# A language-model layer on one core: the gating of four tiles cut in four pieces, and new orders of work on three engines

## The chip, the cores and the metric

The kernel runs on one NeuronCore of a Trainium2 chip. The metric is the device time of one execution in microseconds, as the median of several runs. The core has five engines that run side by side, each taking its own instructions in order: TensorE (PE in the profile; its weight loads are PEld), VectorE (DVE), ScalarE (ACT), GpSimd (POOL) and SyncE (SP, which here only issues DMAs). They wait for one another through semaphores.

## The reference

8192 tokens (64 tiles of 128) pass through three stages; what is computed is this:

```python
h = concat(token_table[ids], cat_table[ids])                      # 256 columns
# linear attention within each of the 64 sequences of 128 tokens, 16 heads of 16
x1 = layernorm(h);  q, k, v = x1 @ W_qkv + b_qkv
pq, pk = elu(q) + 1, elu(k) + 1
h = h + einsum(pq, pk^T v) / (pq . sum(pk) + 1e-6)                # per sequence of 128 tokens
# mixture of 16 experts: cosine logits, those above zero are kept, or the best two
x2 = layernorm(h);  rw = gating(x2, sim_matrix, gates)
q, k, v = sum_e rw_e * x2 @ {q,k,v}_proj[e]
out = h + sum_e rw_e * (softmax(causal(q k^T / sqrt(128))) v) @ o_proj[e]
```

A sequence has 128 tokens, so one tile of 128 rows is one sequence. All of it is in float32; the large products are made of three products of a high and a low half.

## The kernel before

The kernel has three stages. The attention stage gathers the rows of a tile, normalises them, makes q, k and v, the linear attention, the sum `h2`, its normalised form `x2`, and the gating logits; it finds the best two experts of each token, counts how many tokens went to each expert, and scatters each row of `x2` twice, sorted by expert. The second stage multiplies the sorted rows by the experts' weights, and the third does the softmax attention and the output product. Only the attention stage is touched here.

That stage is software-pipelined. `run1` calls `step1` of each engine with c = -7 up to `LAST_STEP`, with no loop left in the program. In step c an engine works on several tiles: `i.shift(n)` is tile c + n. So in one step VectorE makes `phi` of tile c+3, the attention result and `h2` of tile c+2, the low half of the turned `x1` of tile c+4, the statistics of tile c+5, and gating for tiles that have come out. Each engine's order within the step is the order of the code, written out by hand, and `after(eng, step, tile)` waits until another engine has finished that step of that tile.

The ring that goes through every step is this: VectorE writes `roots_in` (L1149, L1150), GpSimd raises it to the power -1/2 (`roots`, L712), VectorE makes `centers` from it (L1102), ScalarE normalises `x1` and `x2` with both (L851, L858), TensorE turns `x1` (L1426), ScalarE copies it as the high half `x1_T` (L864), VectorE makes the low half `x1_lo` (L1124). Then, by VectorE's order and not by need, come the attention result `attn` (L1128), `h2` (L1135), its statistics (L1138, L1140) and the next `roots_in`.

A second ring: from `x1_lo` TensorE makes `qk_product` (L1446 for the bias and six times L1450), ScalarE reads it twice (`qk_negative` L841, `qk_exp` L845), and VectorE makes `phi` (L1108). ScalarE's two come ahead of its `x1_normed` of the next tile. TensorE makes `kv_product` (L1512) from `phi` and from ScalarE's copy `v_copied` (L880), VectorE masks it (`kv_masked`, two instructions at L1160 and L1162), and TensorE makes `attn_sums` from that (L1471). VectorE and ScalarE also split a weight a step (`weight_lo` L511, `weight_hi` L506).

Gating works on groups of four tiles (of two at the end). When the last logits of a group are there, `experts_chosen` runs in that step, `rows_counted` in the next, `rows_placed` in the one after, and in the fourth there is none. They stand in VectorE's order between `roots_in` and `kv_masked`. After `rows_placed` GpSimd scatters one tile a step. Beside this it gathers the rows of tile c+7.

The buffers: `h` has eight, `x2` has nine (`N_X2`), `stats` has four.

## Time and profile before

| | |
|---|---|
| time before, median of 3 runs | 1168.15 us (1163.3 to 1169.42) |
| time of the profiled execution | 1171.71 us |
| its span, first to last instruction | 1170.0 us |
| TensorE busy | 993.7 us (85%) |
| VectorE busy | 861.6 us (74%) |
| GpSimd busy | 703.9 us (60%) |
| ScalarE busy | 603.1 us (52%) |
| attention stage | from the start to about 456 us |
| expert stage | about 456 to 690 us |
| last stage | about 690 us to the end |

The profile gives for each engine its busy time, for each line of the kernel its instructions and what the engine waited for ahead of them, and a timeline. In a timeline a row is: start, duration, engine, line, operation, output and inputs, and in brackets how long the engine had been idle before it and which instruction released it ("issue": nothing that the profile shows). An instruction can start a little ahead of the end of the one before it on its engine, so it is the distance from start to start that adds up. A buffer is sometimes named after another tile that shares its memory: `wo_hi` and `wo_lo` are the attention weights in this stage, `split_hi` and `split_lo` the turned `x1`, `row_y` and `x` are `x1` or `x2`, `h` can be `h2`.

### The profile page before, as it was taken

How to read it: one execution, taken by the hardware profiler on the slowest of the kernel's cores; microseconds unless marked ns; L12 is line 12 of the kernel's file. 1: busy time of each engine (PE TensorE's matmuls, PEld its weight loads, DVE VectorE, ACT ScalarE, POOL GpSimd, SP SyncE). 2: the span in 40 equal slices, each digit the busy share in tenths (PEclk: the TensorE clock that was granted, in tenths of full speed). 3: DMA queues.
4: the chain of work that ended last, by engine and by line, in shares of the span. 5: the costliest groups of instructions: out<-in, count | busy, mean ns of one | idle time of the engine just before them, and what ended most of it. 6: DMA issues, size and time to landing. Idle time of an engine off the chain costs nothing.

```text
span 1170.0 us, 27470 instructions
## 1 busy us (share of the span) xinstructions
PE 993.7 (85%) x6831; PEld 897.0 (77%) x6832; DVE 861.6 (74%) x2889; ACT 603.1 (52%) x1569; POOL 703.9 (60%) x924
## 2 busy tenths in 40 slices
PE   0887888888888871889999959999999999999998
PEld 0675777677776761779898849999999999999997
DVE  2576888888878874645445428888888888888988
ACT  1454666666666640444344425555555555555554
POOL 5666666666666658200000037888888888888885
PEclk9988999999999985899999979999999999999999
DMA  7464333443333323677777752333333333333331
GB/s 204 129 180 123 109 111 124 128 131 118 106 106 110 100 84 128 192 225 235 233 238 229 235 166 82 91 90 90 90 90 91 92 90 90 90 90 90 90 88 35
DMA packets 132265, 149.80 MB, mean 128 GB/s; under 512 B 14708, under 2 KB 119650, under 8 KB 132196
## 3 DMA queue, kind: packets, MB, share of 16 engines
q1 hardware_dynamic: 112964, 97.59, 26.9%
q0 software_dynamic: 18080, 50.36, 14.5%
q10 hardware_dynamic: 1152, 1.05, 0.3%
q8 instruction: 29, 0.48, 0.2%
q14 instruction: 40, 0.33, 0.1%
HBM read 83.79 MB, written 78.88 MB: 139 GB/s over the span
## 4 chain that ended last, share of the span: by engine, by line
PE 25%; POOL 25%; issue 19%; DVE 18%; DMA 5%; ACT 4%; SPq 2%; POOLq 2%; another core or an unknown queue 1%; DVEq 0%; ACTq 0%
POOL row_y L813 6%; PE bank L1419 5%; PE bank L1421 5%; PE bank L1420 5%; PE bank L1426 4%; POOL x2T L798 4%; POOL qk_neg L798 4%; PE bank L1450 3%; POOL x2T L800 2%; POOL qk_neg L800 2%; POOL x2T L794 2%; DVE split_lo L1124 2%; POOL qk_neg L794 2%; DMA h<-in_L_tok_special_table,ids 2%; DVE h L1135 1%
## 5 line engine op out<-in xcount | busy, mean ns | idle before, releaser
L1419 PE MATMUL bank<-wo_hi,split_lo 128*128 128x256 f32 x1024 | 304.4, 297 | 12.8 <-DVE x L1356 6.1
L1421 PE MATMUL bank<-wo_hi,split_hi 128*128 128x256 f32 x1024 | 288.6, 282 | 0.0
L1420 PE MATMUL bank<-wo_lo,split_hi 128*128 128x256 f32 x1024 | 288.2, 281 | 0.0
L1419 PEld LDWEIGHTS bank<-wo_hi,split_lo 128*128 128x128 f32 x1024 | 194.0, 189 | 25.3 <-DVE x L1356 12.2
L1420 PEld LDWEIGHTS bank<-wo_lo,split_hi 128*128 128x128 f32 x1024 | 194.1, 190 | 0.0
L1421 PEld LDWEIGHTS bank<-wo_hi,split_hi 128*128 128x128 f32 x1024 | 193.4, 189 | 0.0
L935 ACT ACTIVATE h<-bank,rwo 128x256 f32<-128x256 f32 x256 | 107.6, 471 | 119.3 <-PE bank L1421 112.6
L813 POOL DMA_INDIRECT row_y<-sorted_y,pair_now x128 | 126.3, 987 | 36.7 <-issue 30.1
L806 POOL COPY pair_now<-pair_at 128x2 uint32 (+1 forms) x64 | 11.9, 186 | 211.0 <-SPq L596 210.9
L1356 DVE SCALAR_TENSOR_TENSOR x<-bank,rwo,x 128x256 f32<-128x256 f32 x256 | 109.0, 475 | 19.7 <-PE bank L1421 19.6
L1257 DVE TENSOR_TENSOR split_lo<-bank,split_hi 128x256 fp32r<-128x256 f32 x144 | 60.9, 424 | 82.3 <-ACT split_hi L897 81.3
L1356 DVE SCALAR_TENSOR_TENSOR qk_e<-bank,rwo,qk_e 128x256 f32<-128x256 f32 x256 | 109.1, 475 | 15.4 <-PE bank L1421 15.1
L1419 PE MATMUL bank<-wq_hi,split_lo 128*128 x288 | 111.1, 386 | 0.0
L712 POOL TENSOR_TENSOR roots<-roots_in,minus_half 128x3 f32<-128x3 f32 x67 | 59.7, 891 | 84.7 <-DVE roots_in L1150 82.7
L740 POOL DMA_INDIRECT sorted_x<-row_y,position_u x86 | 85.5, 994 | 25.9 <-issue 25.9
L1420 PE MATMUL bank<-wq_lo,split_hi 128*128 x288 | 98.4, 342 | 0.0
L1421 PE MATMUL bank<-wq_hi,split_hi 128*128 x288 | 98.3, 341 | 0.0
L897 ACT CAST split_hi<-bank 128x256 fp32r<-128x256 f32 x144 | 54.0, 375 | 72.1 <-PE bank L1426 71.5
L1450 PE MATMUL bank<-wo_lo,split_hi 128*128 128x512 f32 (+1 forms) x256 | 89.9, 351 | 0.0
L1450 PE MATMUL bank<-wo_hi,split_lo 128*128 128x512 f32 (+1 forms) x256 | 89.6, 350 | 0.0
L1450 PE MATMUL bank<-wo_hi,split_hi 128*128 128x512 f32 (+1 forms) x256 | 88.8, 347 | 0.0
L841 ACT ACTIVATE qk_neg<-bank 128x512 f32<-128x512 f32 x64 | 38.3, 598 | 82.3 <-PE bank L1450 70.2
(229 smaller groups left out, 2669.4 us busy)
## 6 DMA issues: line engine op xcount, KB each, us to landing
sorted_y<-row_y SPq DMA_DIRECT2D x36, 384.0 KB, 3.2
sorted_y<-w_attn SPq DMA_DIRECT2D x36, 384.0 KB, 3.2
row_x<-sorted_x SPq DMA_DIRECT2D x72, 128.0 KB, 2.6
h_rows<-h SPq DMA_DIRECT2D x64, 128.0 KB
row_x<-h_rows SPq DMA_DIRECT2D x64, 128.0 KB, 2.1
out_h<-row_x SPq DMA_DIRECT2D x64, 128.0 KB, 1.7
embed_table<-in_L_tok_token_table SPq DMA_DIRECT2D x10, 625.0 KB
embed_table<-in_L_tok_special_table SPq DMA_DIRECT2D x10, 623.0 KB
```

The lines of the kernel that those rows point to most:

```text
L712: pool.tensor_tensor(roots[:, row, :], roots_in[:, row, :], minus_half[:, 0:3], ALU.pow).then_inc(done["roots"], 1)
L740: pool.indirect_dma_start(out=sorted_x, out_offset=offsets(position_u[:, t, n:n + 1]), in_=x2[t % N_X2], in_offset=None).then_inc(scattere ...
L798: pool.tensor_tensor(acc[:, :], part[:, 0, :], acc[:, :], ALU.add).then_inc(o_pooled, 1)
L813: pool.indirect_dma_start(out=row_y[:, 2 * tile.p + n, :], out_offset=None, in_=sorted_y, in_offset=offsets(pair_now[tile.q][:, n:n + 1])) ...
L897: act.copy(split[tile.q][0][:, :, :].rearrange("p c t -> p (c t)"), ps_turn[tile.p][:, 0:C]).then_inc(done["pair_hi"], 1)
L935: last = act.mul(part[:, j, :], ps[:, j * C:(j + 1) * C], rwo[tile.p][:, e:e + 1])
L1257: dve.tensor_tensor(lo, ps_turn[tile.p][:, 0:C], hi.bitcast(F32), ALU.subtract).then_inc(done["pair_lo"], 1)
L1356: ins = dve.scalar_tensor_tensor(acc[j][:, :], src, weight, base[:, :], ALU.mult, ALU.add)
L1419: pe.matmul(ps, left[1][c], right[0][c], start=(c == 0), stop=False)
L1420: pe.matmul(ps, left[0][c], right[1][c], start=False, stop=False)
L1421: last = pe.matmul(ps, left[0][c], right[0][c], start=False, stop=(c == n - 1))
L1450: last = pe.matmul(ps[:, 0:hi - lo], turned[x][c], w_attn_s[w][:, c, lo:hi], start=False, stop=end)
```

## The change

The gating of a group is cut into four functions instead of three, in four steps: `experts_chosen` ends with the best values, the new `experts_numbered` finds their indices and makes the two masks, `rows_counted` keeps the counting, `rows_placed` is as before. Everything behind them moves one step later: the rank product on TensorE, the scatters on GpSimd, and the last step of the stage (`LAST_STEP`), which is one more. `N_X2` is ten instead of nine; the room comes from small tiles that now share memory with others. VectorE's order is new: `weight_lo` goes behind `centers` (a step later than ScalarE's half), `attn` ahead of `x1_lo`, the aggregation of the first statistics ahead of `h2`, `kv_masked` right behind `h2` and so ahead of the statistics of `h2` and of `roots_in`, and the first statistics of a tile are taken at the end of the step before. ScalarE makes `v_copied` ahead of `x1_T`. TensorE makes the logits ahead of turning `x1`, and `kv_product` ahead of `qk_product`.

```diff
-    N_X2, N_RAW = 9, 4
-    LAST_STEP = B + 2
+    N_X2, N_RAW = 10, 4
+    LAST_STEP = B + 3
@@ scatters_at
-                at = first + n + 2
+                at = first + n + 3
@@ ScalarE, step1: behind x2_normed, ahead of x1_T; removed from behind x2_T
+                tile = i.shift(3)
+                if tile.inside(B):
+                    after(act, "v_product", tile)
+                    after(act, "kv_product", tile.shift(-1))
+                    act.copy(vx[:, :, 0:P], ps_v[:, 0:C].rearrange("p (g n) -> p g n", g=G)
+                             ).then_inc(done["v_copied"], 1)
@@ VectorE, gating
-                last.then_inc(gate_own, gate_count("top_values"))
-                gate_wait("top_values")
+                last.then_inc(gate_own, gate_count(f"top_values {g}"))
+
+            def experts_numbered(g):
+                first, n = GROUPS[g]
+                tiles = slice(first, first + n)
+                gate_wait(f"top_values {g}")
                 for t in range(first, first + n):
                     last = dve.max_index(top_at[:, t, :], top[:, t, :], routing[:, t, :])
                 last.then_inc(gate_own, gate_count("top_indices"))
                 gate_wait("top_indices")
-                quad_done(dve, "rank_product", g - 1)
+                quad_done(dve, "position_index", g - 1)
                 (is_one, is_two)
+            def rows_counted(g):
+                quad_done(dve, "rank_product", g - 1)
                 (before_rows, top_two, counts)
@@ VectorE, step1
+                for n in weights_at(i.c - 1):
+                    weight_lo(dve, n)
                 (phi, den)
-                if ln1_tile.inside(B):
-                    rows_landed(dve, ln1_tile.c)
-                    dve.bn_stats(stats[:, 2 * i.p, :], h[ln1_tile.c % 8]).then_inc(done["ln1_stats"], 1)
                 (reciprocal)
-                (x1_lo)
                 (attn)
+                (x1_lo)
+                (bn_aggr of ln1_tile)
                 (h2)
+                (kv_masked: two tensor_tensor, after kv_product of phi_tile)
                 (bn_stats and bn_aggr of h2)
-                (bn_aggr of ln1_tile)
                 (roots_in)
-                for back, piece in ((2, rows_placed), (1, rows_counted), (0, experts_chosen)):
+                for back, piece in ((3, rows_placed), (2, rows_counted), (1, experts_numbered), (0, experts_chosen)):
-                (kv_masked)
-                for n in weights_at(i.c):
-                    weight_lo(dve, n)
+                if stats_tile.inside(B):
+                    rows_landed(dve, stats_tile.c)
+                    dve.bn_stats(stats[:, 2 * (1 - i.p), :], h[stats_tile.c % 8]).then_inc(done["ln1_stats"], 1)
@@ TensorE, step1: the order within a step
-   rank product (i.c - 2), attn_sums, turn x1, logits, turn phi, turn x2, qk_product, kv_product, v_product
+   rank product (i.c - 3), attn_sums, logits, turn x1, turn phi, turn x2, kv_product, qk_product, v_product
```

Words in brackets stand for code that is the same on both sides. `stats_tile` is `i.shift(6)`.

## Rows read from the trace of the kernel before

**Rows 1.** Busy time of each engine in two stretches; columns: stretch, length, engines, clock, DMA.
```profile
121.50:410.20 288.70, 244.73 (x1528) 203.77 (x1528) 239.24 (x1106) 184.14 (x421) 186.38 (x189) 0.99 0.37 114
90.00:109.00 19.00, 12.50 (x65) 10.34 (x66) 9.80 (x47) 7.54 (x17) 11.96 (x13) 0.82 0.45 135
```

**Rows 2.** The same view for L1108 (`phi`, once a step) alone: VectorE busy, count.
```profile
121.50:410.20 288.70, 32.12 (x47) 0.99 0.37 114
```

**Rows 3.** Who waited for whom, 121 to 410 us: total, times, longest.
```profile
POOL roots L712 <- DVE roots_in L1150: 64.3, 47, 2.4
```

**Rows 4.** Timeline of VectorE, one step without gating, from `centers` to `centers`.
```profile
244.61 0.15 DVE L1102 SCALAR_TENSOR_TENSOR centers<-moments,roots 128x2 f32<-128x2 f32 x1
...
245.28 0.17 DVE L1113 TENSOR_SCALAR den<-bank 128x16 f32<-128x16 f32 x1
245.37 0.42 DVE L1118 BATCH_NORM_STATS2 stats<-h 128x6 f32<-128x256 f32 x1
245.70 0.23 DVE L1121 RECIPROCAL zden<-den 128x16 f32<-128x16 f32 x1
246.46 0.42 DVE L1124 TENSOR_TENSOR split_lo<-bank,split_hi 128x256 fp32r<-128x256 f32 x1 [0.53 <-ACT split_hi L864]
246.80 0.41 DVE L1128 TENSOR_TENSOR attn<-bank,zden 128x256 f32<-128x256 f32 x1
247.35 0.43 DVE L1135 TENSOR_TENSOR h<-h,attn 128x256 f32<-128x256 f32 x1
247.81 0.43 DVE L1138 BATCH_NORM_STATS2 stats<-h 128x6 f32<-128x256 f32 x1
...
248.56 0.17 DVE L1149 TENSOR_SCALAR roots_in<-moments 128x2 f32<-128x2 f32 x1
...
249.45 0.43 DVE L1160 TENSOR_TENSOR kvm<-bank,head_mask 128x256 f32<-128x256 f32 x1 [0.67 <-PE bank L1512]
...
250.21 0.15 DVE L1102 SCALAR_TENSOR_TENSOR centers<-moments,roots 128x2 f32<-128x2 f32 x1
```

**Rows 5.** Timeline of VectorE: where the three gating functions begin and end.
```profile
229.84 0.15 DVE L1021 TENSOR_TENSOR energy<-roots 128x4 f32<-128x4 f32 x1
...
231.20 0.09 DVE L1038 MATCH_VALUE_LOAD top_at<-top,routing 128x8 f32 x1
...
231.80 0.40 DVE L1160 TENSOR_TENSOR kvm<-bank,head_mask 128x256 f32<-128x256 f32 x1
...
236.62 0.22 DVE L1048 TENSOR_TENSOR is_one<-expert_no,top_at 128x64 f32<-128x64 f32 x1
...
236.90 0.17 DVE L1055 CAST before_rows<-before_rows 128x16 fp32r<-128x16 f32 x1
...
238.05 0.41 DVE L1160 TENSOR_TENSOR kvm<-bank,head_mask 128x256 f32<-128x256 f32 x1
...
242.88 0.21 DVE L1072 TENSOR_TENSOR ranks<-bank,region_start 128x64 f32<-128x64 f32 x1
...
243.86 0.42 DVE L1160 TENSOR_TENSOR kvm<-bank,head_mask 128x256 f32<-128x256 f32 x1
```

**Rows 6.** Timeline of ScalarE in the step of rows 4.
```profile
244.86 0.60 ACT L851 ACTIVATE x<-h,centers,roots 128x256 f32<-128x256 f32 x1 [0.51 <-DVE centers L1102]
...
246.05 0.37 ACT L864 CAST split_hi<-bank 128x256 fp32r<-128x256 f32 x1
...
248.94 0.60 ACT L841 ACTIVATE qk_neg<-bank 128x512 f32<-128x512 f32 x1 [1.04 <-PE bank L1450]
249.56 0.63 ACT L845 ACTIVATE qk_e<-qk_neg 128x512 f32<-128x512 f32 x1
```

**Rows 7.** Timeline of TensorE and GpSimd in the same step.
```profile
247.03 0.47 PE L1446 MATMUL bank<-bias,ones_r 128*128 128x512 f32 x1 [0.18 <-DVE split_lo L1124]
...
248.87 0.88 POOL L712 TENSOR_TENSOR roots<-roots_in,minus_half 128x3 f32<-128x3 f32 x1 [1.14 <-DVE roots_in L1150]
```

**Rows 8.** Who waited for whom in the starting steps, 33 to 100 us.
```profile
POOL row_x L717 <- DMA row_x<-in_L_tok_special_table,ids: 4.9, 2, 2.6
```

More of the change, by code:

```diff
@@ L269, in build @@
         gates_shifted = wide[0]
+        top_two_f = moments[:, :, :, :].rearrange("p r n m -> p (r n m)")[:, 0:2 * B].rearrange("p (b n) -> p b n", n=2)
+        gap, gates_open = [centers[:, :, :].rearrange("p r n -> p (r n)")[:, n * B:(n + 1) * B] for n in range(2)]
         ids_rows_f, ids_low = qk_e[0:B, 0:T], x2T[:, 0:B]
@@ L875, in step1 @@
                     act.copy(x2T[:, :], ps_x2[:, 0:C]).then_inc(done["x2_T"], 1)
-                tile = i.shift(3)
-                if tile.inside(B):
-                    after(act, "v_product", tile)
-                    after(act, "kv_product", tile.shift(-1))
-                    act.copy(vx[:, :, 0:P], ps_v[:, 0:C].rearrange("p (g n) -> p g n", g=G)
-                             ).then_inc(done["v_copied"], 1)
                 for n in weights_at(i.c):
@@ L1039, in experts_chosen @@
                 last.then_inc(gate_own, gate_count("top_indices"))
-            def rows_counted(g):
-                first, n = GROUPS[g]
-                tiles = slice(first, first + n)
                 gate_wait("top_indices")
-                quad_done(dve, "rank_product", g - 1)
+                quad_done(dve, "position_index", g - 1)
                 numbers = over_quad(expert_no, n)
@@ L1121, in step1 @@
                     dve.reciprocal(zden[:, :, :], den[:, :, :]).then_inc(done["attn_z"], 1)
-                if x1_tile.inside(B):
-                    after(dve, "x1_T", x1_tile)
-                    dve.tensor_tensor(x1T_s[1], ps_x1[:, 0:C], x1T_s[0].bitcast(F32), ALU.subtract
-                                      ).then_inc(done["x1_lo"], 1)
                 if attn_tile.inside(B):
@@ L1131, in step1 @@
                                       ).then_inc(done["attn"], 1)
+                if x1_tile.inside(B):
+                    after(dve, "x1_T", x1_tile)
+                    dve.tensor_tensor(x1T_s[1], ps_x1[:, 0:C], x1T_s[0].bitcast(F32), ALU.subtract
+                                      ).then_inc(done["x1_lo"], 1)
+                if ln1_tile.inside(B):
+                    after(dve, "ln1_stats", ln1_tile)
+                    dve.bn_aggr(moments[:, ln1_tile.c, 0, :], stats[:, 2 * i.p, :]).then_inc(done["ln1_moments"], 1)
+                if attn_tile.inside(B):
                     landed_half(dve, h2_stored, attn_tile.shift(-2))
@@ L1472, in step1 @@
                     last.then_inc(done["attn_sums"], 1)
-                tile = i.shift(4)
-                if tile.inside(B):
-                    after(pe, "x1_lo", tile.shift(-1))
-                    after(pe, "x1_normed", tile)
-                    turn(ps_x1, *halves(x1)).then_inc(done["x1_turned"], 1)
                 if i.inside(B):
@@ L1489, in step1 @@
                     last.then_inc(done["logits_product"], 1)
+                tile = i.shift(4)
+                if tile.inside(B):
+                    after(pe, "x1_lo", tile.shift(-1))
+                    after(pe, "x1_normed", tile)
+                    turn(ps_x1, *halves(x1)).then_inc(done["x1_turned"], 1)
                 tile = i.shift(3)
@@ L1499, in step1 @@
                     turn(ps_x2, *halves(x2[tile.c % N_X2])).then_inc(done["x2_turned"], 1)
-                tile = i.shift(4)
-                if tile.inside(B):
-                    after(pe, "phi", tile.shift(-1))
-                    after(pe, "x1_lo", tile)
-                    if tile.c == 0:
-                        pe.wait_ge(setup_v, 6)
-                    attn_product(tile, ps_qk, 0, 2 * C, "qk_product")
                 tile = i.shift(3)
@@ L1514, in step1 @@
                     last.then_inc(done["kv_product"], 1)
+                tile = i.shift(4)
+                if tile.inside(B):
+                    after(pe, "phi", tile.shift(-1))
+                    after(pe, "x1_lo", tile)
+                    if tile.c == 0:
+                        pe.wait_ge(setup_v, 6)
+                    attn_product(tile, ps_qk, 0, 2 * C, "qk_product")
                 tile = i.shift(4)
```

48 lines of the change are left out of this document (22 added, 26 removed).

## The prediction

> **What bounds the kernel now.** I read the busy time by stretch first, then the waits, then the timeline of single steps. The change touches the attention stage alone; the stages from 456 us on are taken as they are. In the even part of the stage, 121.5 to 410.2 us, 47 steps pass in 288.7 us [rows 1, 2], so a step takes 6.14 us. No engine is full: TensorE is busy 244.7 us of it (85%), VectorE 239.2 (83%), ScalarE and GpSimd 184 to 186 (64%) [rows 1]. So a ring of waits sets the step. GpSimd waited for `roots_in` in every one of the 47 steps [rows 3]: the ring runs over VectorE's `roots_in`.
>
> In a step without gating VectorE needs 5.60 us from `centers` to `centers` (244.61 to 250.21) and stands still twice: 0.53 us ahead of `x1_lo`, which waits for ScalarE's copy of the turned `x1`, and 0.67 us ahead of `kv_masked`, which waits for TensorE [rows 4]. The first of these stands ahead of `attn`, `h2`, its statistics and `roots_in`, none of which need `x1_lo`. And the work is uneven: `experts_chosen` takes 231.80 - 229.84 = 1.96 us, `rows_counted` 238.05 - 236.62 = 1.43, `rows_placed` 243.86 - 242.88 = 0.98, and the fourth step has none [rows 5]. In the long steps VectorE has no second wait to hide the work in; in the fourth it stands idle.
>
> **VectorE's step after the change, from start to start.** I take the step of rows 4 and edit it.
> - It is 5.60 us to begin with.
> - `den` to `reciprocal` was 0.42 with the first statistics between them. Without them the reciprocal waits only for `den` (0.17 long, and a hop of about 0.04): 0.21. The statistics, now at the step's end, take 0.33 (245.37 to 245.70). Together +0.12.
> - `reciprocal` to the next was 0.76, with the wait. `attn` needs the reciprocal's end, 0.23 and a hop: 0.29. That is -0.47.
> - `x1_lo`, `attn`, `h2` took 0.34 + 0.55 = 0.89, where 0.55 is `h2` waiting for `attn`. In the new order `attn`, `x1_lo`, the small aggregation, `h2` take 0.34 + 0.34 + 0.10 = 0.78, for the other two cover the end of `attn`. That is -0.11.
> - `h2` to its statistics was 0.46 by dependence; `kv_masked` between them lets it be 0.34, and its own two instructions and the weight only change place: -0.12.
> - From the second `roots_in` (0.08 behind the first at 248.56) to `kv_masked` was 0.81, mostly the idle 0.67. Now the next instruction follows in about 0.07: -0.74.
> - `x1_lo` could start 1.85 us after `centers` by VectorE's own order (phi, weight, `den`, reciprocal, `attn` ahead of it). ScalarE's `x1_T` started 246.05 - 244.61 = 1.44 after `centers`, and `x1_lo` 0.41 behind it [rows 4, 6]. With `v_copied` put ahead, a copy of the size of L864 (0.37 long), `x1_T` goes to about 1.54 and `x1_lo` to 1.95. So +0.10 of waiting stays.
>
> The sum is 5.60 + 0.12 - 0.47 - 0.11 - 0.12 - 0.74 + 0.10 = 4.38 us and the gating piece of the step. The pieces: choosing to the best values 231.20 - 229.84 = 1.36; numbering 231.80 - 231.20 = 0.60 and the two comparisons 236.90 - 236.62 = 0.28, with two hops 1.0; counting 238.05 - 236.90 = 1.15; placing 0.98 [rows 5]. They are less equal than the words of the change say, but their sum over four steps is 4.49 and the mean 1.12. Nothing of VectorE's time hides them any more. So the mean step by VectorE is 4.38 + 1.12 = **5.50 us** (5.36 at the least, 5.74 at the most).
>
> **Who else could be last.** GpSimd: `roots` started 0.31 after `roots_in` and takes 0.88 [rows 4, 7]; `centers` may start some 1.25 us after `roots_in`. VectorE reaches it after 0.15, a piece of 0.98 or more and statistics of 0.33, thus 1.46. VectorE is later by 0.2 or more in every step, so the power is covered; in the old fourth step nothing but the wait for TensorE covered it.
>
> TensorE, `kv_product`: it needs `v_copied`, which ends some 1.7 us after `centers`, follows the turn of `x2`, and ends at about 2.5; `kv_masked` wants it at 2.76. It is covered by 0.3 us. This is the closest of the moved waits: behind it on VectorE stand the statistics of `h2` and `roots_in`, for which GpSimd waits.
>
> TensorE and ScalarE, the second ring: `x1_lo` to the start of `qk_product` 247.03 - 246.46 = 0.57, to `qk_negative` 248.94 - 247.03 = 1.91, to `qk_exp` 0.62, to `x1_normed` 0.54 (its 0.63 less the usual overlap), from there to `x1_T` 246.05 - 244.86 = 1.19 and 0.10 for `v_copied`, and 0.41 to `x1_lo` [rows 4, 6, 7]. That makes 5.34 us a step, 0.16 less than VectorE. `kv_product` ahead of `qk_product` costs this ring nothing, since it runs while TensorE waits for `x1_lo`. The logits ahead of the turn of `x1` run while it waits for `x1_normed`. TensorE's own work is 244.7 / 47 = 5.2 us a step as busy time, with overlapping matmuls in it, so it is no bound by itself but leaves little room.
>
> GpSimd's work is 186.4 / 47 = 3.97 us a step and some 0.8 us between its indirect DMAs [rows 1]: 4.8, covered. The scatters go one step later and the tenth `x2` buffer gives that step back, so ScalarE's wait for a free buffer has the same number of steps as before. SyncE's DMAs keep their places; the store of `h2` follows `h2`.
>
> **The sum.** In the even part 47 x (6.14 - 5.50) = 30.1 us are saved. The start: rows of the first tiles come in parts, and GpSimd waits up to 2.6 us for a DMA there [rows 8], so these steps gain nothing; the first statistics, now one step nearer to the DMA that they need, may wait in some of them. Between -1 and +5 us, I take +1. The steps between start and even part ran in part at the low clock, two of them in 19.0 us at a mean granted clock of 0.82 [rows 1]; I take a gain of 1 us there. The end: one more step, which holds almost no work, but the last groups are placed one step later while GpSimd has scatters queued: between 0 and 5.6 us (a whole step), I take 1. Together 30.1 - 1 + 1 - 1 = 29 us. The profiled execution took 1171.71 us, hence 1142.6; it lies 3.6 us above the median of the runs shown, hence **1139 us**.
>
> **A rule weighed.** While GpSimd raises the roots, VectorE runs gating instructions with two inputs in SBUF; in the new order it does so in four steps of four instead of three. In the trace the counting step shows no stretching: 1.43 us for `rows_counted` is the sum of its short instructions, beside a `roots` of the usual length [rows 5, 7]. The Trainium skill says (SBUF — State Buffer, SBUF: two separate sides) that VectorE with two SBUF inputs and a GpSimd instruction that reads SBUF exclude each other for a whole instruction. By that rule the fourth step would pay a `roots` too, and it is the third rival below; the trace speaks against it.
>
> **Rivals.**
> 1. The second ring or `kv_masked` is last (25%). Its margins are 0.16 and 0.3 us, and the hops in it were read from an order in which they were not tight. If each of its six hops is 0.07 us longer, the step is 5.75: 47 x 0.39 = 18 us, and the time is 1150.
> 2. VectorE's step is shorter than the sum, because satisfied waits cost it less than in the old order, and low-clock spells vanish with TensorE's pauses (15%). With 5.36 a step and 3 us for the spells the time is 1129.
> 3. VectorE and GpSimd exclude each other (3%): 0.88 us more in one step of four, 47 x 0.22 = 10 us back: 1149.
> 4. The early steps are held by the DMA of the small table (3%): each of about 14 steps loses the 2.6 us of rows 8, 36 us, which takes all the gain: 1175, slower. Its place is the first statistics at the step's end, its point is a landing more than a step after the issue. Against it: the statistics have one step more than the landing needs once VectorE and GpSimd run over two steps.
> 5. TensorE's clock falls more often (5%). Two steps in 19.0 us [rows 1] make 9.5 a step at the low clock, 4 us more than 5.5. From 8 such steps on, the gain is gone; with 12 the time is 1139 + 48 = 1187, slower. Against it: the granted clock is 0.99 over the even part [rows 1], and the change shortens TensorE's pauses.
> 6. The stage gets faster but the end takes it back, the scatters being late anyway (5%): within 0.5%.
>
> **Chances.** The forecast as it stands 44%, the rivals as given. The measurement of this kernel can tell about 0.5% (5.8 us) from no change. Faster by more: 0.87; within: 0.05; slower: 0.08. The range takes in rivals 1 to 3 and VectorE's own bounds: 1127 to 1156.
>
> **What would show it.** In the trace after, starts of `phi` 5.3 to 5.7 us apart in all four steps of a group, 22.0 us for the four. The idle time ahead of `x1_lo` at 0.1 us instead of 0.53, the one ahead of `kv_masked` gone, and VectorE busy for over 90% of the even part. GpSimd still waits for `roots_in`, but `centers` does not wait for GpSimd. If `kv_masked` or `phi` shows idle time with TensorE or ScalarE as its releaser, rival 1 holds; if the first statistics wait for a DMA in many steps, rival 4; if the clock row shows more low slices, rival 5. The prediction is wrong if the step stays above 5.9 us, that is, if one of the moved waits is as late as the one it replaces.

## The result and the profile after

The changed kernel took **1125.18 us** (median of 4 runs, 1122.11 to 1129.77), the kernel before 1167.62 us (4 runs, 1163.3 to 1169.42): ratio 0.9637, 95% interval 0.9597 to 0.9677. The forecast was 1139 us with 1127 to 1156 as its range, so the gain was larger than forecast and the time lies below the range. That number needs a caution: of the four later sessions in which the changed kernel ran, it took 1149 and 1157 us in two, every run of it, beside an unchanged kernel before. The experiments find out what it is exposed to there.

The page of the profiled execution of the changed kernel (1126.18 us, span 1124.4): first line of the page, then VectorE's and the clock's row in 40 slices.

```profile
span 1124.4 us, 27485 instructions
...
DVE  2578999999999746454544279999999999988798
...
PEclk9999999999999859999999789999999999999899
```

From its fifth slice to the end of the even part VectorE is busy for nine tenths and more of the time, where it was at eight before. The same stretch as [rows 1], from step 10's `phi` to step 57's: columns stretch, length, PE, PEld, DVE, ACT, POOL, clock, DMA. The second line is `phi` alone (the stretch's end catches one more than 47), the third the 19 us in which [rows 1] had a clock of 0.82.

```profile
109.64:361.60 251.96, 233.33 (x1533) 202.44 (x1532) 236.63 (x1106) 170.68 (x422) 184.51 (x189) 1.00 0.42 131
...
109.64:361.60 251.96, 32.35 (x48) 1.00 0.42 131
...
90.00:109.00 19.00, 15.40 (x90) 12.95 (x89) 15.03 (x72) 10.46 (x27) 12.92 (x13) 0.91 0.38 118
```

47 steps in 251.96 us are **5.36 us** a step instead of 6.14. VectorE is busy for 236.63 / 251.96 = 94% of it and TensorE for 93%. Who waited for whom in that stretch:

```profile
ACT qk_neg L840 <- PE bank L1456: 77.4, 47, 2.0
POOL roots L711 <- DVE roots_in L1163: 28.9, 46, 1.1
...
ACT x L850 <- DVE centers L1106: 0.7, 2, 0.4
```

VectorE, which stood 0.53 us ahead of `x1_lo` in the steps before, is all but gone from this list (0.3 us ahead of `phi`, in one step). GpSimd's wait for `roots_in` fell from 64.3 us [rows 3] to 28.9. One step of VectorE, to be read beside [rows 4]:

```profile
221.58 0.14 DVE L1106 SCALAR_TENSOR_TENSOR centers<-moments,roots 128x2 f32<-128x2 f32 x1
...
222.65 0.17 DVE L1119 TENSOR_SCALAR den<-bank 128x16 f32<-128x16 f32 x1
222.85 0.26 DVE L1123 RECIPROCAL zden<-den 128x16 f32<-128x16 f32 x1
223.14 0.42 DVE L1126 TENSOR_TENSOR attn<-bank,zden 128x256 f32<-128x256 f32 x1
223.49 0.42 DVE L1132 TENSOR_TENSOR split_lo<-bank,split_hi 128x256 fp32r<-128x256 f32 x1
223.82 0.17 DVE L1136 BATCH_NORM_AGGREGATE moments<-stats 128x2 f32<-128x6 f32 x1
223.91 0.39 DVE L1141 TENSOR_TENSOR h<-h,attn 128x256 f32<-128x256 f32 x1
224.22 0.42 DVE L1147 TENSOR_TENSOR kvm<-bank,head_mask 128x256 f32<-128x256 f32 x1
224.56 0.17 DVE L1149 TENSOR_TENSOR kvm<-bank,head_of_row 128x16 f32<-128x16 f32 x1
224.64 0.42 DVE L1154 BATCH_NORM_STATS2 stats<-h 128x6 f32<-128x256 f32 x1
...
225.45 0.15 DVE L1163 TENSOR_SCALAR roots_in<-moments 128x1 f32<-128x1 f32 x1
225.52 0.15 DVE L1020 TENSOR_TENSOR energy<-roots 128x4 f32<-128x4 f32 x1
...
226.77 0.41 DVE L1172 BATCH_NORM_STATS2 stats<-row_x 128x6 f32<-128x256 f32 x1
227.09 0.14 DVE L1106 SCALAR_TENSOR_TENSOR centers<-moments,roots 128x2 f32<-128x2 f32 x1
```

No instruction carries an idle time in brackets. From `centers` to `centers` it is 5.51 us, of which the choosing piece has 226.77 - 225.52 = 1.25.

That doesn't mean that VectorE never waits. An instruction of 256 columns is 0.42 us long here and the next one starts 0.34 after its start, so a wait of up to 0.08 us hides in the overlap. It is seen by the distance from the releasing instruction. ScalarE's copy and `x1_lo`, in the step above and in the next one:

```profile
223.09 0.37 ACT L869 CAST split_hi<-bank 128x256 fp32r<-128x256 f32 x1
...
228.58 0.37 ACT L869 CAST split_hi<-bank 128x256 fp32r<-128x256 f32 x1
...
228.57 0.42 DVE L1126 TENSOR_TENSOR attn<-bank,zden 128x256 f32<-128x256 f32 x1
228.98 0.42 DVE L1132 TENSOR_TENSOR split_lo<-bank,split_hi 128x256 fp32r<-128x256 f32 x1
```

`x1_lo` starts 0.40 us behind the start of the copy and 0.03 behind its end, in both steps and in each of the 47; it is the same 0.03 in the kernel before, where VectorE stood idle for it. So the copy still releases it. In the second step `attn` to `x1_lo` is 0.41 us instead of 0.34: 0.07 us of waiting. On the average of the even steps this hidden wait is 0.04 us. `phi` has one too. In the choosing step it starts 0.10 us behind the end of ScalarE's `qk_exp`, the least that any step of any of these kernels has, and about 0.08 later than VectorE could start it; that is 0.03 us on the average of all steps.

The two profiled executions, 1171.71 and 1126.18 us, differ by 45.5 us: 11.9 up to step 10 (`phi` at 121.55 and 109.64), 36.7 in the 47 even steps, 3.8 from there to the start of the last stage (687.12 and 634.69), and 6.8 lost in the last stage. Part of that is chance: three profiles of the kernel before have step 10 at 121.55, 113.00 and 115.18 and a last stage of 482.9, 488.3 and 481.3 us; three of the changed kernel have 109.64, 109.94 and 109.48, and 489.7, 488.2 and 489.1. The even part is the same in all: 6.142, 6.141 and 6.142 against 5.361, 5.360 and 5.362 us a step.

### The profile page after: what moved, and what is told of

Same layout as the page of the kernel before. It is cut to its first block, busy times and chain, and to the rows that moved or that the text cites. A ratio compares the mean times of both kernels' runs of the same rounds, so it can differ in the third digit from the quotient of the medians.

```text
span 1124.4 us, 27485 instructions
## 1 busy us (share of the span) xinstructions
PE 981.4 (87%) x6831; PEld 895.2 (80%) x6832; DVE 878.1 (78%) x2889; ACT 585.5 (52%) x1569; POOL 709.3 (63%) x924
## 4 chain that ended last, share of the span: by engine, by line
POOL 27%; DVE 23%; PE 22%; issue 18%; DMA 5%; SPq 2%; POOLq 2%; ACT 1%; DVEq 0%; ACTq 0%
POOL row_y L812 6%; PE bank L1425 6%; PE bank L1427 5%; PE bank L1426 5%; POOL x2T L797 4%; PE bank L1432 3%; POOL qk_neg L797 3%; DVE phi L1114 3%; DMA h<-in_L_tok_special_table,ids 2%; POOL x2T L799 2%; POOL qk_neg L799 2%; POOL x2T L793 2%; POOL qk_neg L793 2%; DVE kvm L1147 2%; DVE attn L1126 2%
## 5 line engine op out<-in xcount | busy, mean ns | idle before, releaser
L812 POOL DMA_INDIRECT row_y<-sorted_y,pair_now x128 | 128.8, 1006 | 36.7 <-issue 29.3
L739 POOL DMA_INDIRECT sorted_x<-row_y,position_u x80 | 79.8, 997 | 24.1 <-issue 23.8
```

Source lines behind the costliest of these rows:

```text
L739: pool.indirect_dma_start(out=sorted_x, out_offset=offsets(position_u[:, t, n:n + 1]), in_=x2[t % N_X2], in_offset=None).then_inc(scattere ...
L812: pool.indirect_dma_start(out=row_y[:, 2 * tile.p + n, :], out_offset=None, in_=sorted_y, in_offset=offsets(pair_now[tile.q][:, n:n + 1])) ...
```

## The experiments

Five sessions after that of the result, each on one chip; the second, third and fourth on the same one by its number. The kernel before took 1168.06, 1170.34, 1168.85, 1165.6 and 1168.11 us in them.

**The two halves of the change.** `orders_only` is the changed kernel with the old cut of the gating:

```diff
-                for back, piece in ((3, rows_placed), (2, rows_counted), (1, experts_numbered), (0, experts_chosen)):
+                for back, piece in ((2, rows_placed), (1, rows_counted), (0, experts_chosen)):
```

What hangs on the cut goes back with it (`LAST_STEP`, the scatters, the rank product); `N_X2` stays ten.

> The changed kernel with the gating back in three pieces (1.96, 1.43, 0.98 us and none). Theory, VectorE's own order sets each step and rings only fill up the short one: steps of about 6.2, 5.7, 5.3 and 5.3 us, 5.6 on average instead of 5.34, so 47 x 0.27 = 13 us more than the changed kernel: 1138 us. Rival, the rings through TensorE and ScalarE set the mean and the pieces only move work: the mean step stays at 5.3 to 5.4 and the time at 1125 us.

`pieces_only` is the kernel before with the new cut:

```diff
-                for back, piece in ((2, rows_placed), (1, rows_counted), (0, experts_chosen)):
+                for back, piece in ((3, rows_placed), (2, rows_counted), (1, experts_numbered), (0, experts_chosen)):
```

Here `N_X2` is ten too, and the rest moves a step later as in the change.

> The kernel before with the gating in four pieces and everything that moves with them, in the old orders. Theory: a piece of about 1.1 us in each step costs what it exceeds the 0.7 us of waiting for kv_product by, so the steps are about 6.1, 6.0, 5.9, 5.8, 5.96 on average instead of 6.14, 7 to 8 us less than before: 1160 us. Rival, the pieces were most of the gain: under 1145 us. Second rival, they gain nothing without the orders: 1167 us.

Measured: 1140.77 us (ratio 0.9767, 0.9748 to 0.9786; mean step 5.638) and 1151.08 us (0.987, 0.9841 to 0.9899; mean step 5.901). The orders alone bring 27.3 us, the pieces alone 17.0, and the whole change 42.1 in that session (one run, `after_again`, 1125.95; `before_again`, one run for its trace, took 1163.78): nearly the sum. For `pieces_only` the expectation was 9 us too high; it had put the steps at 6.1, 6.0, 5.9 and 5.8 us, and they were 6.07, 5.81, 5.89 and 5.82.

> The kernel before once more, for its trace. If the spells of low TensorE clock in the first 111 us (five in the first trace) belong to the kernel, there are three or more again, and the first 13 steps take about 88 us again (from phi at 33.75 to phi at 121.55). If they are chance, their number differs and the time to that point moves by 5 us or more.

> The changed kernel once more, for its trace. If the 12 us gained by step 10 belong to the change, phi of that step starts at about 110 us again; if they were chance of the clock, it moves by 5 us or more. The even steps take 5.34 us again. The last stage, 6.8 us longer than before in the first trace, comes back to within 2 us of the 482.9 us of before if its extra low-clock spell was chance.

In `orders_only` the four kinds of step take 6.15, 5.69, 5.32 and 5.26 us from `phi` to `phi`. VectorE's order without a piece is 4.26 us, the short wait for `x1_T` in it, so with 1.96, 1.43 and 0.98 it would be 6.22, 5.69, 5.24 and 4.26. The last two are longer than that: something else ends them. Two starts of `phi` in `orders_only` show it:

```profile
222.19 0.69 DVE L1109 SCALAR_TENSOR_TENSOR phi<-bank,qk_e 128x512 f32<-128x512 f32 x1
227.44 0.69 DVE L1109 SCALAR_TENSOR_TENSOR phi<-bank,qk_e 128x512 f32<-128x512 f32 x1 [0.21 <-ACT qk_e L844]
```

`phi` waits for ScalarE's `qk_exp`: that is the second ring of the prediction, measured at 5.25 us where it was put at 5.34. A long step can't be made up by a short one below it, and this is what the equal pieces are worth once the orders are new.

**VectorE or the second ring.** `dve_plus` adds one instruction of 0.42 us to VectorE's step, `stats_mid` puts the first statistics back where they stood:

```diff
+                    dve.bn_stats(extra[:, i.p, :], h[stats_tile.c % 8])
```

> The changed kernel with one more bn_stats of 256 columns on VectorE at the end of each step, into a tile that nobody reads. Theory, VectorE's own work is the step: the even steps grow by the 0.33 us that such an instruction takes from start to start, from 5.36 to 5.69 on average, and the time by 16 us. Rival, the ring through TensorE and ScalarE (5.27 us by the trace) sets it: under 0.15 us a step more.

```diff
@@ VectorE, step1
                 (phi, den)
+                if ln1_tile.inside(B):
+                    rows_landed(dve, ln1_tile.c)
+                    dve.bn_stats(stats[:, 2 * i.p, :], h[ln1_tile.c % 8]).then_inc(done["ln1_stats"], 1)
                 (reciprocal ... gating)
-                if stats_tile.inside(B):
-                    (the same for stats_tile)
```

> The changed kernel with the first statistics back between den and the reciprocal. It fills a gap of 0.12 us of VectorE, so by VectorE's work alone a step falls to 5.24 us. By the second ring (phi to x1_lo 1.45 us by VectorE's order, then 0.56, 1.91, 0.63 and 0.69 us through TensorE and ScalarE back to phi: 5.24) it makes phi to x1_lo 0.21 longer, and no step can be under 5.45. If both rules hold the average is 5.5, slower than the 5.36 of the changed kernel; if the first alone, 5.24.

`dve_plus` took 1140.44 us with a mean step of 5.664, 0.30 more for an instruction that takes 0.33 from start to start. The missing 0.03 is the wait ahead of `phi`, which is gone there; `x1_lo` still starts 0.03 us behind the end of ScalarE's copy in every step. So what closes the mean step is a mixed ring: `centers`, by ScalarE and TensorE to `x1_T` and `x1_lo` (1.89 us), then VectorE's own order to the next `centers`. VectorE's own way to `x1_lo` is only 0.06 us shorter there. `stats_mid` took 1132.27 us, and nearly all its steps are 5.44 to 5.47 us from `phi` to `phi`, whatever piece they hold (the longest has 5.57); its `phi` waits:

```profile
223.19 0.69 DVE L1114 SCALAR_TENSOR_TENSOR phi<-bank,qk_e 128x512 f32<-128x512 f32 x1 [0.20 <-ACT qk_e L844]
```

With 0.22 us more between `phi` and `x1_lo` (`den` to `reciprocal` is 0.42 instead of 0.20) the second ring is last in every step. Without them it is about 5.22 to 5.25 us, 0.1 below the changed kernel's mean. The margin isn't there in each step: in the changed kernel `phi` starts 0.10 us behind the end of `qk_exp` in the choosing, counting and placing steps (medians 0.10, 0.10 and 0.11), which is the least there is, and only behind a choosing step has it 0.28. `act_idle` and `act_ring` add a copy to ScalarE's step, at its end and between `v_copied` and `x1_T`:

```diff
@@ ScalarE, step1, in one at the end, in the other ahead of x1_T
+                if 0 <= i.c < B - 4:
+                    act.copy(x1T[:, :], zeros[:, :])
```

> The changed kernel with one more copy of 256 columns on ScalarE (0.27 to 0.4 us) at the end of its step, where it stands idle for 1.6 us waiting for qk_product. Both theories: no change, 5.36 us a step, 1125 us. If ScalarE's work were a bound, 0.3 us a step more.

> The changed kernel with the same copy between v_copied and x1_T. VectorE reaches x1_lo when x1_T is just ready, so the 0.27 us (start to start) come back as standing still ahead of x1_lo, in VectorE's row and in both rings: 5.6 to 5.65 us a step, 12 us more, 1137 us. If x1_T had slack (the prediction had x1_lo wait 0.10 us, so it had none either), no change.

They took 1156.96 and 1161.05 us in the third session, where late signals (below) disturb about half of the steps. The undisturbed ones are 5.50 and 5.32 us in `act_idle`, 5.82 and 5.64 in `act_ring`: 0.3 us for the same copy, only because of its place, and `x1_lo` stands idle for 0.29 us in `act_ring`. So `x1_T` has no slack, while the end of ScalarE's step has. The times of the whole runs say nothing here.

**The moved instructions of VectorE.** `attn_late` puts `x1_lo` ahead of `attn` again, `kvm_late` puts `kv_masked` behind the gating:

```diff
+                (x1_lo)
                 (attn)
-                (x1_lo)
```

> The changed kernel with x1_lo ahead of attn again. x1_T is ready 0.35 us after VectorE gets there, so it stands still, and h2 then waits for the end of attn (0.2): the even steps grow by 0.4 to 0.55 us, to 5.8 to 5.9, and the time by 19 to 26 us. If ScalarE's wait is hidden anyway, 0.1 us or less.

```diff
                 (h2)
-                (kv_masked)
                 (bn_stats and bn_aggr of h2, roots_in, gating)
+                (kv_masked)
```

> The changed kernel with kv_masked back behind the gating piece. VectorE's work is the same and kv_product is ready in both places, and attn_sums still has 0.3 us before den wants it: the same time within 0.1 us a step, 1121 to 1130 us. If the move of kv_masked was what took away the waits, 0.3 us a step or more slower.

`attn_late` took 1149.5 us, mean step 5.848. This is the wait of [rows 4], back again:

```profile
224.87 0.42 DVE L1126 TENSOR_TENSOR split_lo<-bank,split_hi 128x256 fp32r<-128x256 f32 x1 [0.44 <-ACT split_hi L869]
```

So `attn` ahead of `x1_lo` is worth 5.848 - 5.360 = 0.49 us a step, 23 us in all; the forecast had -0.47 for this wait. `kvm_late` took 1132.93 us, mean step 5.470, 0.11 more: `h2` to its statistics is 0.43 us there (222.34 to 222.77) where with one instruction between it could be 0.31. `kv_masked` ahead of `roots_in` is worth that little, if TensorE is on time.

**The same kernel, 30 us slower.** `filled_gaps` moves `bn_aggr` and half of `kv_masked` into short dependence waits; `after_timed` is the changed kernel beside it.

```diff
-                (bn_aggr of ln1_tile)
                 (h2, kv_masked's first instruction)
+                (bn_stats of h2)
                 (kv_masked's second instruction)
-                (bn_stats of h2)
                 (bn_aggr of h2)
+                (bn_aggr of ln1_tile)
```

> The changed kernel with two short instructions of VectorE moved into gaps of dependence: the second of kv_masked (0.08 us) between the statistics of h2 and their aggregation, the aggregation of the first statistics (0.09 us) between that and roots_in. VectorE's work falls from 5.36 to 5.19 us a step, the rings stay at 5.24 to 5.27. Theory with both bounds: 5.27 to 5.29 us a step, 3 to 4 us less than the changed kernel: 1121 us. By VectorE alone: 5.19, 8 us less. If the gaps were not free: no change.

> The changed kernel as it is, on the same chip as filled_gaps: 1125 us, and even steps of 5.36 us.

`filled_gaps` took 1150.91 us (0.9855, 0.9832 to 0.9878) and the changed kernel 1157.36 (0.9907, 0.9887 to 0.9928; 6 runs, 1154.79 to 1159.6). Both expectations fell. `filled_gaps` was 6.4 us below the changed kernel beside it (mean step 5.783 against 5.915), but in a session with late signals that can't be put down to the filled waits. The undisturbed steps of `after_timed` are the known 5.3 and 5.5 us, but others take 5.9 and 6.9; in them VectorE waits ahead of `kv_masked`, which it never did in the even part of the profile after. The fourth session was to tell whether `kv_masked`'s place is what pays. `kvm_late_timed` is `kvm_late` again, `vcopy_late` is this:

```diff
@@ ScalarE, step1
-                (v_copied)
                 (x1_T, phi_q_T, x2_T)
+                (v_copied)
```

> The changed kernel itself once more. Theory A (what made it 1157 us in the third job belongs to that job): 1125 us, steps of 5.3 and 5.4 us, and no wait of kv_masked for kv_product beyond 0.1 us. Theory B (the kernel has two levels, met by chance of the job): 1157 us, with steps of 5.9 to 6.9 us among steps of 5.3, each with kv_product's signal 2 us and more behind the start of its matmuls.

> The changed kernel with kv_masked moved from ahead of the second statistics to the end of VectorE's step. If TensorE's signals are on time in this job: 1133 us, as in the second job (mean step 5.47). If they are late in some steps, theory A says that a late kv_product signal of 1 to 1.5 us no longer stops roots_in and the gating, so this kernel is faster than the changed kernel in the same job: 1135 to 1142. Theory B (late signals cost whatever the order, since x1 turned and phi turned are late as well): as slow as the changed kernel, 1155 to 1165.

> The changed kernel with ScalarE's v_copied (0.39 to 0.42 us) put back behind the copies of x2, where it stood before. Nothing on VectorE's ring or the second ring waits for it unless kv_product becomes late: kv_product follows it on TensorE, and kv_masked follows kv_product on VectorE. Theory: kv_product is done about 1.2 us later in the step, and kv_masked waits up to 0.5 us for it: mean step 5.36 to 5.9, 1125 to 1150 us. Rival: the copy fits into ScalarE's idle time and nothing moves: 1125 us.

> The kernel before, for its trace on this chip: 1163 to 1170 us, mean step 6.14. Where TensorE's signals are late in this job, they are late here too, and cost little, since kv_masked stands last in VectorE's step.

Measured in that session: the changed kernel 1149.01 us (ratio 0.9852, 0.9825 to 0.9878), `kvm_late_timed` **1130.46** (0.9692, 0.9668 to 0.9716), `vcopy_late` 1185.57 (1.0184, 1.0143 to 1.0225), the kernel before 1168.15 with a mean step of 6.142. The changed kernel's step of 5.888 and VectorE in one of the bad ones:

```profile
230.77 0.43 DVE L1126 TENSOR_TENSOR attn<-bank,zden 128x256 f32<-128x256 f32 x1
231.53 0.42 DVE L1132 TENSOR_TENSOR split_lo<-bank,split_hi 128x256 fp32r<-128x256 f32 x1 [0.34 <-ACT split_hi L869]
231.87 0.17 DVE L1136 BATCH_NORM_AGGREGATE moments<-stats 128x2 f32<-128x6 f32 x1
231.96 0.39 DVE L1141 TENSOR_TENSOR h<-h,attn 128x256 f32<-128x256 f32 x1
233.45 0.42 DVE L1147 TENSOR_TENSOR kvm<-bank,head_mask 128x256 f32<-128x256 f32 x1 [1.09 <-remote]
```

and TensorE's matmuls for it ("remote": the profile has no record of the releasing signal; it is `kv_product`, L1511):

```profile
230.51 0.41 PE L1432 MATMUL bank<-ident,phi 128*128 128x128 f32 x2
...
231.01 0.64 PE L1511 MATMUL bank<-vx,phi 128*128 128x130 f32 x4
```

The matmuls end at 231.65 by their row, and `kv_masked` starts 1.80 us later. The cleanest view is one kernel in two sessions, `kvm_late` and `kvm_late_timed`, a step of each. TensorE's turn of `phi` and ScalarE's work around the copy `pqT` that reads it, first in the second session:

```profile
221.25 0.41 PE L1432 MATMUL bank<-ident,phi 128*128 128x128 f32 x2
...
221.51 0.37 ACT L869 CAST split_hi<-bank 128x256 fp32r<-128x256 f32 x1
221.78 0.38 ACT L874 COPY pqT<-bank 128x256 f32<-128x256 f32 x1
...
224.38 0.60 ACT L840 ACTIVATE qk_neg<-bank 128x512 f32<-128x512 f32 x1 [1.65 <-PE bank L1456]
```

then in the fourth:

```profile
221.86 0.40 PE L1432 MATMUL bank<-ident,phi 128*128 128x128 f32 x2
...
222.14 0.37 ACT L869 CAST split_hi<-bank 128x256 fp32r<-128x256 f32 x1
223.56 0.38 ACT L874 COPY pqT<-bank 128x256 f32<-128x256 f32 x1 [1.04 <-PE bank L1432]
...
225.02 0.60 ACT L840 ACTIVATE qk_neg<-bank 128x512 f32<-128x512 f32 x1 [0.51 <-PE bank L1456]
```

From the start of the turn to `pqT` it is 0.53 us in the one and 1.70 in the other; to `qk_neg` 3.13 and 3.16. TensorE started its work at the same times, and only the signals in the middle of the step came late. I worked out the same from the trace's records of the signals: how long after the last matmul's recorded end its signal came, over 121 to 361 us. "Seen" is how many of the signals have a record; some are missing, most of them in the traces with late ones, so "none late" holds for those seen. The last row is the trace that the prediction was worked from.

```
kernel (session)   turn of phi                kv_product                 mean step
                   seen   median  90%   most  seen   median  90%   most
changed (1)        45/45  0.01   0.01   0.01  45/45  0.01   0.01   0.01  5.360
kvm_late (2)       44/44  0.01   0.01   0.01  44/44  0.01   0.01   0.01  5.470
changed (3)        28/40  0.01   0.96   1.37  38/40  0.82   1.78   1.80  5.915
changed (4)        28/41  0.01   0.62   0.97  35/41  0.76   1.68   1.73  5.888
kvm_late (4)       34/44  0.13   0.58   1.27  44/44  1.35   1.42   1.52  5.484
vcopy_late (4)     27/38  0.01   0.01   0.01  28/37  0.01   0.01   0.04  6.393
before (4)         27/39  0.01   0.01   0.49  39/39  0.01   0.01   0.01  6.142
changed (5)        45/45  0.01   0.01   0.01  45/45  0.01   0.01   0.01  5.362
before (first)     31/39  0.01   0.01   0.56  39/39  0.01   0.01   0.01  6.142
```

In the fourth session `kv_product` is late by 1.35 us in the median with `kv_masked` last in the step, and that costs 5.484 - 5.470 = 0.01 us a step; it is late by 0.76 with `kv_masked` ahead of `roots_in`, and that costs 5.888 - 5.360 = 0.53. So it is by `kv_masked`'s place that the changed kernel pays for late signals, as theory A had it for `kvm_late_timed` (it was even less, 1130 for 1135 to 1142). Its other half, that only the third session has this level, was wrong: the changed kernel met its higher level again, as theory B had it for `after_fourth`. What makes the signals late is open: the kernel before has two late turns of `phi` and no late `kv_product` in the same session, the mean granted clock is 0.96 to 0.97 with and without them, and `kvm_late` has none in the second session on the same chip. The changed kernel itself ran on that chip in the two sessions with late signals only; that it is the session and not the chip is known from `kvm_late` alone.

`vcopy_late` failed in the other direction, by more than the 0.5 us of its expectation, with TensorE's signals on time. One step of it, ScalarE, TensorE, VectorE:

```profile
227.71 0.41 ACT L879 COPY vx<-bank 128x256 f32<-128x256 f32 x1
...
228.16 0.49 PE L1511 MATMUL bank<-vx,phi 128*128 128x130 f32 x2 [0.80 <-ACT vx L879]
...
228.99 0.42 DVE L1147 TENSOR_TENSOR kvm<-bank,head_mask 128x256 f32<-128x256 f32 x1 [0.85 <-PE bank L1511]
```

The late copy holds `kv_product`; this one stands ahead of `qk_product` on TensorE now, so the second ring is held too (`qk_product` starts 1.32 us behind `x1_lo`, 0.57 in the changed kernel), and `kv_masked` stands ahead of `roots_in`, so the first one is. Without the early `v_copied` the kernel is 1.8% slower than before. Of the two moves that lean on it only `kv_masked`'s was taken back singly (`kvm_late`, 0.11 us a step more); TensorE's order was not.

**A kernel with both.** `kvm_mid` puts `kv_masked` between `roots_in` and the gating, and `bn_aggr` of the first norm between `h2` and its statistics.

```diff
-                (bn_aggr of ln1_tile)
                 (h2)
-                (kv_masked)
+                (bn_aggr of ln1_tile)
                 (bn_stats and bn_aggr of h2)
                 (roots_in)
+                (kv_masked)
                 (gating)
```

> The changed kernel with kv_masked moved from ahead of the second statistics to right behind roots_in, and with the first norm's bn_aggr between h2 and the second statistics, so that the 0.11 us that bn_stats waits behind h2 when it follows at once is filled. VectorE's own work per step is unchanged. If TensorE's signals are on time: mean step 5.36 to 5.40, 1125 to 1128 us. If kv_product's signal comes 3.3 us behind phi's start, as in the fourth job: roots_in is issued about 3.2 us behind it, so kv_masked waits 0 to 0.2 us instead of about 1.1, and GpSimd's roots are not held at all: mean step 5.4 to 5.55, 1127 to 1134 us, against 1149 to 1157 of the changed kernel. Rival (the early places of both kv_masked and v_copied do not matter, and the late signals stop something else): 1145 or more.

> The changed kernel itself in the same job. 1125 us if TensorE's signals are on time in it, 1149 to 1157 if they are late as in the third and fourth; the theory that the extra time is kv_masked's wait wants mean step 5.9 only together with kv_product signals over 1 us late.

1127.88 us (0.9644, 0.9623 to 0.9665), mean step 5.404, beside 1127.06 us (0.9642, 0.9614 to 0.967) of the changed kernel. Signals were on time in the fifth session, so it shows that this order costs at most 0.04 us a step, but not that it withstands late signals; that stays untried. `kv_masked` starts 1.22 us behind `kv_product`'s recorded end there, and 0.27 in the changed kernel, so a signal up to about 0.9 us late should hold it no more than one on time does in the changed kernel (an estimate, the difference of these two distances). Of what was run, `kvm_late` is the order to keep where the level has to be sure: 1132.93 and 1130.46 us in the two sessions, against 1125 to 1157 of the changed kernel.

## Why the prediction was wrong, point by point

The mechanism was right and so was the sign; sizes were off, and one argument failed, that the starting steps gain nothing. The forecast saved 29 us; the three profiles of each kernel differ by 41.4 on average, the medians by 42.4. Of the 12.3 us between 29.1 and 41.4, VectorE's step has 6.6, the start 6.9, the end 3.7, and the last stage -4.9.

- **VectorE's step: forecast 5.50 us, measured 5.36.** This is 6.6 of the missing us. Term by term, from start to start, measured as the mean of the 47 even steps:

| term | forecast | measured |
|---|---|---|
| `den` to `reciprocal` | 0.21 | 0.20 |
| `reciprocal` to `attn` | 0.29 | 0.29 |
| `attn`, `x1_lo`, `bn_aggr`, without the wait | 0.78 | 0.77 |
| `h2` to the next | 0.34 | 0.32 |
| second `roots_in` to the next | 0.07 | 0.06 |
| first statistics at the end | 0.33 | 0.33 |
| wait ahead of `x1_lo` | 0.10 | 0.04 |
| wait ahead of `phi` | none | 0.03 |
| choosing, numbering, counting, placing | 1.36, 1.0, 1.15, 0.98 | 1.25, 1.00, 1.06, 0.98 |
| mean piece | 1.12 | 1.07 |
| step without a piece | 4.38 | 4.29 |

No single term failed. The largest miss is the **+0.10 for waiting ahead of `x1_lo`**. It came from a row of the old order: ScalarE's copy with `v_copied` ahead at 1.54 us after `centers`, `x1_lo` 0.41 later at 1.95, and VectorE there at 1.85. After, the copy (L869) starts 1.50 us after `centers` on average, `x1_lo` 1.90, and VectorE's own way there is 1.86. So the wait was foreseen, and it is there; but its size is the small difference of two long sums, and an error of 0.05 us in one of them halves it. The pieces give 0.05 us more, choosing and counting being 0.1 shorter each, and hundredths in `h2` and other terms the rest.
- **Low-clock spells**: the granted clock over the even part went from 0.99 to 1.00. Rival 2 had the step (5.36) and this right, and at 1129 us it was the nearest case. It was given 15%. It had VectorE's step shorter than the sum in general, and so it was: several terms came out short by 0.01 to 0.11 us.
- **The start: forecast 0 (-1 for the first statistics, +1 for the spells), measured about 7.** Step 10 comes at 109.7 us on average of three profiles, against 116.6. `orders_only` has it at 110.1 and `pieces_only` at 114.3, so most of it belongs to the orders. The argument that these steps gain nothing because rows of the first tiles come late was the failed step: GpSimd still waits for its DMA (3.7 and 3.6 us in the starting steps), the first statistics wait 4.7 us in all for theirs, and the steps are shorter all the same. By step 6 the gain is 3.2 us, and the four steps from there to step 10 give 3.7 more, 0.9 each, much as even steps do. Part of it is the clock: from the first `phi` to step 10 the mean granted clock is 0.90, 0.96 and 0.94 in the three profiles before, 0.98, 0.96 and 0.98 in those after. In the profiled execution that I worked from, this part had been slow by chance (121.55, others 113.0 and 115.2).
- **The end: forecast -1, measured +2.7** from step 57 to the last stage; the three profiles before span 9 us there (272.1 to 281.2), so the extra step costs nothing that can be told from chance. **The last stage: forecast 0, measured -4.9** (484.2 us on average before, 489.0 after), with the same instructions. The other traces show that this isn't the change: `before_again` has 488.3 too, the changed kernel has 485.1 and 482.4 in the third and fourth sessions, and `kvm_late` 487.2 and 482.1. A spell at the lower clock level between 1040 and 1090 us goes with the longest ones: all seven traces that have it lie at 488.2 to 489.7, the thirteen without at 481.3 to 487.2. So, as far as these traces tell, the 4.9 us belong to which executions were profiled and not to the change.
- **The second ring: forecast 5.34, measured 5.25**, last in the steps with short pieces in `orders_only` and in nearly all steps of `stats_mid`. Rival 1 had its hops 0.07 us longer than read; they were a little shorter. The ring stayed 0.1 us behind the mean step, but it holds the choosing step's `phi` by 0.08, where the prediction gave it 0.16 in every step. The sign that was to show all this, idle time in the profile, could not: waits under 0.08 us don't appear in it.
- **`kv_product` covered by 0.3 us**: shown in the profile after (`kv_masked` starts 0.27 us behind `kv_product`'s recorded end on average, 0.21 at the least) and called the closest of the moved waits. What was behind it was named too: the statistics of `h2`, `roots_in`, and GpSimd. But the prediction gave a late signal no case of its own, and the sessions of 1149 and 1157 us are that case. No signal of `kv_product` is late in the kernel before (0.01 us at most), and its `kv_masked` stood where such a delay costs little. But the trace that the prediction was worked from had a hint: two of its 31 recorded signals of the turn of `phi` are late, one by 0.56 us.
- **GpSimd and VectorE side by side** (rival 3): `roots` is 0.88 us long in every step, whatever runs beside it. Of counting's additions with both inputs in SBUF (L1068, 109 to 400 us), 36 ran wholly inside a `roots` and 20 not, and both kinds are 0.18 us long; the counting step takes 5.32 us from `centers` to `centers`. The rule of the Trainium skill (SBUF — State Buffer, SBUF: two separate sides) would have made it 0.88 longer (an estimate: the length of one `roots`). The trace doesn't bear it out here.
- **Rivals 4 to 6** did not occur: no step lost 2.6 us to the small table, and the clock did not fall more.
- **The range** ended at 1127, 2 us above the result. It was built from the bounds of VectorE's step and rivals 1 to 3; the start had no bound that let it gain, though a single execution, partly at the low clock, was its only source.

## What to carry to other kernels

Cut the work that has no deadline into pieces such that the engine's step with each piece is just above the next ring, and find that ring before: here two rings lay within 0.1 us of VectorE's own work. Look for them by the distance from the releasing instruction's end, since a wait shorter than the overlap of two instructions is in no idle time. When a wait is moved ahead of what closes the ring, ask not only whether the row shows it covered, but what it costs when the signal is a microsecond late; an instruction that nobody needs soon is cheap insurance at the end of the step (0.11 us a step here, against 0.53). Orders on several engines that depend on each other are judged together, and the start of a pipeline is read from more than one execution.

## What the runs showed of the hardware

**TensorE's signals can come up to 1.8 us behind its matmuls.** In two of five sessions, `kv_product`'s signal came a median of 0.6 to 1.4 us (by kernel) behind the recorded end of its matmuls, while the next matmuls started at their usual times and the signal of `qk_product`, 2 us later, was on time again. The Trainium skill (Perfetto Trace Analysis, Tensor Engine Instruction) says that the end in the profile is estimated from the instruction's size, and that the signal is sent only once PSUM has acknowledged all bytes. The rows agree in so far as the row of a matmul doesn't show the delay and the waiting engine's does; which part of the way is late no run here shows.

**The same program on the same chip can have it in one session and not in another**: `kvm_late` has no late signal in the second and all of `kv_product`'s late in the fourth. The changed kernel's 6 and 4 runs of its two sessions all lie at the higher level, and kernels with another order beside it have hardly any late signal (`vcopy_late`, and the kernel before). A single session of close runs is no proof of a kernel's level: the 95% intervals of the first result (0.9597 to 0.9677) and of the third session (0.9887 to 0.9928) exclude each other.

**VectorE waits without idle time.** An instruction of 256 columns is 0.42 us long and the next starts 0.34 us after it when nothing holds it, so waits under 0.08 us leave no gap; here they are up to 0.07 us ahead of `x1_lo` and 0.08 ahead of `phi`.

**Small VectorE instructions with two inputs in SBUF ran inside GpSimd's `roots` unstretched**, 0.18 us inside and outside.
